# A fused recurrent block and 64-expert MoE on one core: the shared-expert work moved one group earlier, and a merge of the first sequence's token picks added

## The reference

```
x = x + recurrent(layernorm(x))          # projections, cumulative sum over time, norm, output projection
h = layernorm(x);  logits = h @ w_router.T;  top 4 experts per token, softmax weights
for each expert e: take the FIRST 64 tokens that chose it (C = 64)
    y = (silu(h[tok] @ w_gate[e]) * (h[tok] @ w_up[e])) @ w_down[e] * weight;   x[tok] += y
x = x + (silu(h @ sh_gate) * (h @ sh_up)) @ sh_down       # shared expert, all 2048 tokens
```

## Time and profile before

| | |
|---|---|
| median of 3 runs | 709.67 us (709.3 to 709.78) |
| the profiled execution | 709.67 us, its span 707.8 us |
| PE busy | 667.0 us, 94% of the span |
| DVE busy | 325.7 us, 46% |
| POOL busy | 219.5 us, 31% |
| ACT busy | 161.1 us, 23% |
| transfers | 202.67 MB, mean 286 GB/s |

### The profile page before, as it was taken

One profiled execution on the slowest core, in us unless ns is written; L12 is line 12 of the kernel. 1 busy time (PEld: TensorE's weight loads), 2 busy tenths in 40 slices (PEclk: granted clock), 3 DMA queues, 4 the chain that ended last, 5 costly groups with the idle time before them and its releaser, 6 DMA issues. The chain is left out here.

```text
span 707.8 us, 8987 instructions
## 1 busy us (share of the span) xinstructions
PE 667.0 (94%) x3227; PEld 402.9 (57%) x3227; DVE 325.7 (46%) x784; ACT 161.1 (23%) x259; POOL 219.5 (31%) x209
## 2 busy tenths in 40 slices
PE   3999999999999998999999999999999999999980
PEld 2587878878878754444555455455455445444430
DVE  5887567859958771332332323233222323323220
ACT  4833114623211411121211211111111112112110
POOL 4637546535558131022222112221220202220121
PEclk9999999999999999999999999999999999999996
DMA  8201015722775987599999999999999999999972
GB/s 325 68 1 60 1 31 178 267 76 92 295 290 194 355 309 275 205 374 387 389 405 403 386 372 385 394 400 396 367 392 393 402 357 401 388 402 387 371 240 39
DMA packets 52347, 202.67 MB, mean 286 GB/s; under 512 B 7331, under 2 KB 7459, under 8 KB 51920
## 3 DMA queue, kind: packets, MB, share of 16 engines
q1 hardware_dynamic: 36512, 169.23, 60.2%
q0 software_dynamic: 8928, 21.33, 12.7%
q10 hardware_dynamic: 6864, 11.54, 4.4%
HBM read 178.66 MB, written 23.59 MB: 286 GB/s over the span
## 5 line engine op out<-in xcount | busy, mean ns | idle before, releaser
L626 POOL DMA_INDIRECT out_dram<-ym,midx x32 | 51.3, 1602 | 301.7 <-DVE ym L1233 121.7
L1569 PE MATMUL bank<-w_sb,xT 128*64 128x384 f32 x768 | 129.1, 489 | 0.8 <-ACT xT L849 0.8
L1357 PE MATMUL bank<-x_hi,w_parts 128*128 128x512 f32 x368 | 116.5, 400 | 4.1 <-DVE x_lo L962 3.2
L1590 PE MATMUL bank<-w_sb,guT 128*64 128x512 f32 x384 | 88.0, 593 | 2.3 <-DMA w_sb<-in_L_ffn_w_down 2.0
L1569 PEld LDWEIGHTS bank<-w_sb,xT 128*64 128x64 f32 x768 | 53.0, 137 | 63.8 <-issue 60.1
L1357 PEld LDWEIGHTS bank<-x_hi,w_parts 128*128 128x128 f32 x368 | 70.5, 192 | 20.5 <-DVE x_lo L962 4.0
L1357 PE MATMUL bank<-x_lo,w_parts 128*128 128x512 f32 x184 | 71.4, 397 | 0.0
L1173 DVE TENSOR_TENSOR gu<-sg,bank 128x384 f32<-128x384 f32 x32 | 17.7, 554 | 114.5 <-issue 107.7
L1490 PE MATMUL bank<-sh_sb,xS 128*128 128x384 f32 x192 | 63.9, 486 | 0.0
L1590 PEld LDWEIGHTS bank<-w_sb,guT 128*64 128x64 f32 x384 | 27.6, 137 | 51.0 <-issue 50.2
L1490 PEld LDWEIGHTS bank<-sh_sb,xS 128*128 128x128 f32 x192 | 35.7, 191 | 22.3
(11 more groups left out here) (181 smaller groups left out, 949.1 us busy)
## 6 DMA issues: line engine op xcount, KB each, us to landing
w_sb<-in_L_ffn_w_down SPq DMA_DIRECT2D x64, 768.0 KB
w_sb<-in_L_ffn_w_gate SPq DMA_DIRECT2D x48, 768.0 KB
w_sb<-in_L_ffn_w_up SPq DMA_DIRECT2D x48, 768.0 KB
extra<-in_L_ffn_w_gate SPq DMA_DIRECT2D x16, 768.0 KB
extra<-in_L_ffn_w_up SPq DMA_DIRECT2D x16, 768.0 KB
ring<-in_L_attn_x SPq DMA_DIRECT2D x14, 256.0 KB, 3.8
xt_dram<-xwT ACTq DMA_DIRECT2D x12, 256.0 KB, 3.4
xS<-xt_dram SPq DMA_DIRECT2D x12, 256.0 KB, 17.9
```

What stands on the lines that cost most here:

```text
L626: pool.indirect_dma_start(out=out[:, :], out_offset=bass.IndirectOffsetOnAxis(ap=midx[j % 3][u][:, :], axis=0), in_=ym[u][:, :], in_offset ...
L1357: ins = pe.matmul(ps[u][:, :], w, xp, start=(n == 0), stop=(n == len(parts) - 1))
L1569: ins = pe.matmul(ps[e * C:(e + 1) * C, 0:I], xT[:, c, e * C:(e + 1) * C], gate_up(2 * j + u, e, k)[:, c, :], start=(c == 0), stop=(c == K ...
L1590: ins = pe.matmul(pair_bank(j, u)[e * C:(e + 1) * C, :], guT[0][:, c, e * C:(e + 1) * C], down(2 * j + u, e)[:, c, :], start=(c == 0), sto ...
```

## The change

There are two edits.

The first takes `FIRST` away: the 12 shared tiles run in groups 1 to 12 instead of 2 to 13, so group 1 gets one and group 13 has none. The batches of `yS` move along, to groups 3, 6, 9 and 12. SP loads each later `xS` tile one group earlier, and the pairs whose result is split into two parts for the merge (`in_parts`) are (0,0) to (12,0) and (0,1) to (11,1) instead of (0,0), (2,0) to (13,0) and (1,1) to (12,1): 25 pairs both times.

The second edit is in the first part. The first sequence's winners go to `best` and are then merged across the two halves at once: `move_best(0)` on PE, directly behind PE's step 13, brings the upper half down; DVE puts both into `cand` (64 partitions x 128) and runs eight more rounds on it, four after its step 13 and four after step 14 (`merge_rounds`). Their 64 winners stand behind the second sequence's keys on partitions 0 to 63; on 64 to 127 this room is filled with -1. The later rounds and `move_best(1)` stay.

```diff
-FIRST = 2
...
-        def has_shared(j):
-
-            return j == 0 or FIRST <= j < FIRST + SHARED
...
-                first, last, shared = j == 0, j == GROUPS - 1, has_shared(j)
+                first, last, shared = j == 0, j == GROUPS - 1, j <= SHARED
...
-        BATCHES = range(FIRST + 2, FIRST + SHARED, 3)
+        BATCHES = range(3, SHARED + 1, 3)
...
+            def halves_together():
+
+                seq.then(dve.tensor_copy(cand[:, 0:C], best[0:E, :]))
+                dve.wait_ge(best_moved, 1)
+                seq.then(dve.tensor_copy(cand[:, C:], ps_t[1][0:E, 0:C]))
+
+            def merge_rounds(rounds):
+
+                for k in rounds:
+                    found = key[0:E, HALF + 8 * k:HALF + 8 * k + 8]
+                    seq.then(dve.max(found, cand[:, :]))
+                    if k < C // 8 - 1:
+                        seq.then(dve.match_replace(cand[:, :], found, cand[:, :], -1.0))
...
                 elif s == STEPS + 5:
+                    halves_together()
+                    merge_rounds(range(4))
+                elif s == STEPS + 6:
+                    merge_rounds(range(4, 8))
+                    seq.then(dve.memset(key[E:P, HALF:], -1.0))
+
                     seq.then(dve.tensor_scalar(ramp[:, :], ramp[:, :], -float(T), None, ALU.add))
...
-            def move_best():
-
-                pe.wait_ge(best_ready, 1)
-                pe.matmul(ps_u[0][0:E, 0:C], ident[:, E:P], best[:, :], start=True, stop=True).then_inc(best_moved, 1)
+            def move_best(b):
+
+                pe.wait_ge(best_ready, b + 1)
+                pe.matmul((ps_t[1], ps_u[0])[b][0:E, 0:C], ident[:, E:P], best[:, :], start=True, stop=True).then_inc(best_moved, 1)
...
+                if s == STEPS + 5:
+                    move_best(0)
```

More of the change, by code:

```diff
@@ L170, in moe_block @@
         best = tile("best", [P, C])
+        cand = tile("cand", [E, 2 * C], at=xin_at + 1024)
         slots = tile("slots", [E, C], at=xin_at + 512)
@@ L474, in _ @@
                     load_down(p - 2)
-                if p % 2 and 2 <= (p - 1) // 2 - FIRST < SHARED:
-                    load_shared_tile((p - 1) // 2 - FIRST)
+                if p % 2 and 2 <= (p - 3) // 2 < SHARED:
+                    load_shared_tile((p - 3) // 2)
                 for k in range(2):
@@ L865, in shared_out @@
                 if t >= 3 and t % 3 == 0:
-                    act.wait_ge(added, landed(t + FIRST - 1, 0) + ADD)
+                    act.wait_ge(added, landed(t, 0) + ADD)
                 act.activation(yS[:, t % 3, :], ps_d[1][:, :], ACT.Copy).then_inc(yS_ready, 1)
@@ L883, in group @@
                 if shared:
-                    silu_shared(item(j))
+                    silu_shared(j + (LEAD - 1))
                 if first:
@@ L895, in group @@
                 elif shared:
-                    shared_out(j - FIRST)
+                    shared_out(j - 1)
             def shared_turn_copy(t):
@@ L1063, in best_rounds @@
                 for k in rounds:
-                    found = best[:, 8 * k:8 * k + 8] if b else key[:, HALF + 8 * k:HALF + 8 * k + 8]
-                    if b and k == C // 8 - 1:
-                        dve.max(found, keys).then_inc(best_ready, 1)
[L1067 to L1071, removed]
+                    found = best[:, 8 * k:8 * k + 8]
+                    if k < C // 8 - 1:
+                        seq.then(dve.max(found, keys))
+                        seq.then(dve.match_replace(keys, found, keys, -1.0))
+                    else:
+                        dve.max(found, keys).then_inc(best_ready, 1)
+                        dve.wait_ge(best_ready, b + 1)
             def weight_sums(b):
@@ L1530, in _ @@
             late_product(2, 0)
-            move_best()
+            move_best(1)
             turn_shared(1, ps_xt)
@@ L1549, in merge_pair @@
                 if in_parts(j, u):
-                    pe.wait_ge(ylow_ready[u], sum(in_parts(i, u) for i in range(j + 1)))
+                    pe.wait_ge(ylow_ready[u], j + 1)
                     pe.matmul(pair_bank(j, u)[:, :], same[u][:, :], y[:, :], start=True, stop=False)
```

21 lines of the change are left out of this document (10 added, 11 removed).

## The result

The changed kernel takes **715.83 us** (median of 4 runs, 714.2 to 717.33) against 709.48 (4 runs beside it, 708.58 to 709.78): a ratio of 1.0089, 95% interval 1.0062 to 1.0116. It is slower, as forecast, but by 6.35 us where 2.0 were predicted, and it lies outside the predicted range. Three more executions on record took 713.75, 716.94 and 719.23 us.

A forecast was written before the change was run, and what follows sets the result against it. The end was taken as bound by POOL's non-overlapping scatters, whose start PE sets, with PE and transfers full behind. 709.67 + 3.0 (added PE wait) - 1.0 (earlier last batch) = 711.7 us; range 709.0 to 714.0.

The forecast's parts named there:

- The merge rounds: DVE behind steps 13 and 14: 0.73 us a round over 128 columns, hidden behind waits for PE, so nothing was added.
- The four steps around the last batch: POOL's row of scatters near the end: four steps including a batch take 44.75 us, as around group 10's batch.
- one more scatter under load: POOL's row before (14, 0): one further scatter while weights are loaded takes 9.5 us.
- (14, 0) won: End of the kernel: with the earlier batch, the scatter of (14, 0) is issued 1.8 us earlier, before the +3.0 shift.
- PE's stall on `ym`: Down product of (14, 0) waits some 1.8 us for DVE's copy of (13, 1), covered by later waits.
- the term of 3.0 us for the added wait: PE behind step 13: 2.5 us standing still, 0.41 move, some 0.1 hand-over; passed on whole to the expert stage.
- The bounds, 2.2 to 3.4: Limits of the +3.0: PE's position at 188.2 and 0.2 for the matmul; or 0.3 us for the restart.
- rival 4: PE restarts slowly after the pause: eight microseconds at half pace cost 4 us, 715.7 us in all; chance 0.04.
- a gap in the weight stream: Group 1 with a shared tile frees weight room up to 7.2 us later; gap bounded 0 to 1 us, taken 0.
- 1.0 was taken for the batch: Last batch one group earlier: 1.8 us won under load, worth 1.1 at the end, rounded to 1.0; bounds 0 to 2.3.
- the first edit's sum, -1.0: First edit's whole effect: 0 for the tile in group 1, 1.0 us gained by the earlier last batch.

The follow-up runs named there:

- the wait alone: Kernel before, plus only one 64-column PE matmul behind step 13 that waits for DVE's last round, result unused, no merge: 715.83 us, ratio 1.0099.
- a plain 2.5 us: Kernel before, plus eleven unused 128x512 matmuls (2.5 us) behind PE's step 13, no wait: 711.88 us, ratio 1.0034.
- the merge alone: Kernel before, plus only the second edit (merge with its wait on PE), shared tiles in groups 2 to 13 as before: 715.49 us, ratio 1.0090.
- first edit with gates first: First edit only, with SP loading gate and up of pairs 5 and 6 ahead of the down parts of pairs 3 and 4: 709.24 us.
- the wait filled by busy work: Second edit only on the kernel before, plus 18 unused matmuls (4.1 us) on PE ahead of the waiting move: 714.36 us, ratio 1.0065.

## Why the prediction was wrong, step by step

**Right.** The added wait sets the loss, and nothing takes it back: the wait alone gave all of it within the noise, and a plain 2.5 us were passed on as 2.5. PE was at the border at 188.0 (187.7 predicted). The merge rounds cost 0.70 us each (0.73) and are hidden. Groups 2 to 12 start 7.2 us later by the tile. The four steps around the last batch took 45.3 us (633.39 to 678.71; 44.75), one more scatter under load 9.4 (9.5), and (14, 0) won 1.3 (1.8). PE's stall on `ym` for the down product of (14, 0) was 1.6 us (1.8).

**The step that failed is the term of 3.0 us for the added wait.** In the merge alone the same place cost 5.2 us up to step 14's sums (201.49 against 196.28), in the profiled changed kernel 8.89. Two parts of the term were wrong. The slow restart was left out of it; that part is shown best, and in the profiles of the merge alone and the wait alone it is the larger. The length of the wait is the other part.

**The length: "PE would stand still from 187.7 to 190.2, that is 2.5 us".** The 2.5 was read from one trace as if DVE's last round had one time. PE's wait was 3.04 us in the merge alone and 3.09 in the wait alone, within the bounds, and 6.38 in the profiled changed kernel. Up to this round all fourteen kernels of this case do the same work, and it starts at 188.9 to 191.2 us in twelve of the traces and at 193.35 and 193.65 in the other two. Three whose first part is that of before (first edit with gates first, the half version without a tile in group 2, the one without a tile in group 12):

```profile
189.34 0.69 DVE L1081 MAX8 key<-key 128x8 f32<-128x512 f32 x1
```

```profile
191.15 0.69 DVE L1077 MAX8 key<-key 128x8 f32<-128x512 f32 x1
```

```profile
193.35 0.70 DVE L1077 MAX8 key<-key 128x8 f32<-128x512 f32 x1
```

The 189.52 of before is 0.5 us ahead of the middle one (190.0), so it was no odd trace; what it could not show is the tail of some 4 us behind it. There nobody waits for that round: DVE has 2.25 us of waiting left at step 14 and 3.88 at step 15, which take such a lag up. The added wait makes PE's time depend on it. It fits that the changed kernel's 4 runs lie 3.1 us apart and those of the wait alone 3.9, against 1.2 for the 4 runs of before beside the changed kernel and 1.3 for the 4 with the wait filled by busy work (27 runs of before lie 2.2 apart). The bounds, 2.2 to 3.4, held PE's side of the uncertainty and none of DVE's.

**The restart: rival 4, given 0.04, and put at 0.3 in the bounds.** It is real here. It cost 1.8 us behind a pause of 3.04 us and about 2 behind 6.38, and the clock rows show its cause. The row that suggested it was not a good witness: the matmuls at the start of the kernel were twice as slow at a granted clock of 1.00 (15 to 20 us), so by that row it was something else, and behind the pause of 2.00 us at 681.50 the matmuls were as fast as ever. That rival 4 named the right mechanism from it was in part luck; the rule of the Trainium skill that the prediction cites beside it was the better ground. Its price was twice what was measured (4 us, for 8 us at half the pace).

**The third: a gap in the weight stream, "I bound a gap there at 0 to 1 us and take 0".** A tile in group 1 costs 1.8 us. The earlier end, last tile and last batch, gives 1.8, where 1.0 was taken for the batch (bounds 0 to 2.3). The two terms cancel, and the first edit's sum, -1.0, came out as 0.1.

Put together by medians: 6.1 for the second edit and 0.1 for the first are 6.2 of the measured 6.35. Of the 6.1, the merge alone's profile has 3.0 of wait, 0.3 of the move and 1.8 of restart, together 5.1 at group 1. Of the missing 1.0, 0.3 are lost behind group 1 in that profile (715.05 against 709.67); the rest is that it is 0.4 faster than its own median, and the profile of before 0.25 slower than the 709.42 beside it. How long PE waited in the other runs is not recorded. For the changed kernel's median, 715.83, the split between wait and restart stays open therefore; only its profiled execution, 3.4 us above the median, is known to have waited 6.38.

**What stays open.** Why DVE's scan and product took 2.00 and 1.57 us in some places and 1.28 and 0.69 in others: POOL worked on its own 128x512 operands at the time and was slow too (2.17 us for a product that took 1.29 in before), but no experiment separated them. The Trainium skill (GPSIMD Engine Reference, 1. Specifications) says that the two engines share their way to the on-chip memory and that a DVE instruction with two operands there contends with POOL; the rows fit it, since it is the scan and the product of two operands there (L975) that grew, and neither the MAX8 between them nor the product that reads a bank (L967, 0.67 to 0.69 throughout). And why the profiles with the first edit lose 0.4 us (alone) and 1.1 us (changed kernel, with either place of the move) between group 1 and the last scatter, where the first edit's median shows 0.1.

## What to carry to other kernels

A semaphore from an engine that lags unseen is not free to wait for: read how late the producer may be over several executions, and place the consumer behind work that the waiting engine has anyway (here one line, two products later, gives back 5.0 of the 6.35 us). To the length of a pause on PE add the restart, here about 1.8 us behind 3 us of pause (a pause of 2.0 us at 681.50 showed none); busy work of 4.1 us moved group 1 less than a wait of 3.0, 3.9 us against 5.1. And where a stream of loads is full, look at its first microseconds: the order in which the room is asked for was worth 1.6 us, as much as moving the work that frees it.

## What the runs showed of the hardware

- PE behind a pause: granted clock 0.57 in the first 3.9 us after 3.04 us of pause, 0.65 in the first 6 us after 6.38, and 1.00 where matmuls filled the pause. An x_lo matmul of 128x512 showed 0.63 us instead of 0.39.
- MAX8 over 128 columns of 64 partitions took 0.29 us and MATCH_REPLACE8 0.27, with 0.08 more for loading its values.
- On DVE a scan of 128x512 took 1.22 to 2.22 us, and a product `r_sb` of two on-chip operands 0.69 to 1.61, in the same kernel.
- An accumulating scatter of one pair took 9.3 to 9.5 us from issue to issue under the full weight stream, and 5.6 to 6.2 when it is over (702.71 and 708.90 in the changed kernel).
